# Reordering a few steps of a four-engine software pipeline: third tile's scale, two bias sums, third q's transpose, first z, and a score copy

## What is computed

```
# block 0: modulated linear, per-token attention among 16 heads of 32, modulated linear
kx = x @ (w * style * demod).T + b ; q = k = v = kx as (B, N, 16, 32)
A  = softmax(q @ k^T / sqrt(32))            # 16 x 16 for each token
x  = x + modulated_linear(A @ v)
# block 1: six normalised or shifted copies of x, one wide MLP, layer norm
h = ln(ln(x) * pw_g[id1] + pw_b[id1]) * cp_g[id2] + cp_b[id2] ; t, s = ln(x) * g[id] + b[id]
m, n, r = x + small MLPs of three conditioning vectors
x = x + ln(silu(concat(w0*h, w1*t, w2*m, w3*n, w4*r, w5*s) @ W1 + b1) @ W2 + b2) * g + be
```

## Time and profile before

| | |
|---|---|
| median of 3 runs | 898.75 us (898.54 to 901.41) |
| the profiled execution, its own time | 895.99 us |
| its span, first to last instruction | 894.2 us |
| TensorE busy | 849.9 us (95%) |
| VectorE busy | 699.7 us (78%) |
| GpSimd busy | 631.7 us (71%) |
| ScalarE busy | 482.4 us (54%) |
| mean granted TensorE clock | 0.984 of full speed |

### The profile page before, as it was taken

How to read it: one execution, slowest core, us unless ns; L and a number is a source line. 1 busy time by engine, 2 the same in 40 slices (tenths; PEclk the granted TensorE clock), 3 DMA queues, 4 the chain that set the end, 5 groups by cost and what they waited for, 6 DMA issues and landing times.

```text
span 894.2 us, 19747 instructions
## 1 busy us (share of the span) xinstructions
PE 849.9 (95%) x7456; PEld 770.7 (86%) x7474; DVE 699.7 (78%) x1099; ACT 482.4 (54%) x851; POOL 631.7 (71%) x766
## 2 busy tenths in 40 slices
PE   5996788999999999999999999999999999999987
PEld 5854777999899898999899898999899898999976
DVE  3687767779897878778897877789897877778642
ACT  3566446465555646465555646465555646464531
POOL 2458795868877776868878766868877776857661
PEclk9897999999999999999999999999999999999999
DMA  8961232434443341324444342434333342322110
GB/s 297 417 230 51 59 89 72 112 73 141 101 130 101 84 113 49 113 71 143 101 125 107 84 113 49 115 71 142 100 109 98 84 111 50 102 70 79 42 49 25
DMA packets 104367, 95.56 MB, mean 107 GB/s; under 512 B 72880, under 2 KB 78160, under 8 KB 102608
## 3 DMA queue, kind: packets, MB, share of 16 engines
q1 hardware_dynamic: 95056, 69.26, 26.8%
q0 software_dynamic: 4608, 16.78, 6.6%
q10 hardware_dynamic: 4608, 8.25, 2.7%
HBM read 69.60 MB, written 8.40 MB: 87 GB/s over the span
## 4 chain that ended last, share of the span: by engine, by line
PE 61%; DVE 16%; POOL 9%; issue 6%; ACT 4%; DMA 2%; ACTq 1%; SPq 0%; another core or an unknown queue 0%; DVEq 0%; POOLq 0%
PE acc L392 28%; PE tok L392 22%; PE att L392 5%; PE xp L545 4%; PE xp L392 2%; DVE Wkl L1151 2%; DVE SE L1288 1%; POOL op0l L1648 1%; DMA kb<-in_kb 1%; DVE op0l L1350 1%; DVE q L1251 1%; ACT L892 1%; DVE SE L1273 1%; DVE small L1284 1%; DVE xb L1312 1%
## 5 line engine op out<-in xcount | busy, mean ns | idle before, releaser
L1648 POOL TENSOR_TENSOR op1l<-ytmp,op1h 128x512 fp32r<-128x512 f32 x64 | 85.7, 1339 | 14.5 <-ACT op1h L880 13.9
L1594 POOL TENSOR_TENSOR xlo<-xraw,xhi 128x512 fp32r<-128x512 f32 x31 | 42.9, 1382 | 52.1 <-ACT xhi L775 52.1
L392 PE MATMUL acc<-op0h,W1xh 128*128 128x256 f32 x256 | 75.7, 296 | 3.8 <-DVE op0l L1330 3.4
L392 PE MATMUL acc<-op1h,W1th 128*128 128x256 f32 x256 | 75.6, 295 | 0.0
L880 ACT CAST op1h<-ytmp 128x512 fp32r<-128x512 f32 x64 | 39.7, 620 | 64.8 <-DVE ytmp L1344 64.8
L392 PE MATMUL acc<-op1h,W1hh 128*128 128x256 f32 x256 | 73.7, 288 | 0.0
L392 PE MATMUL acc<-op0h,W1sh 128*128 128x256 f32 x256 | 73.7, 288 | 0.0
L392 PE MATMUL acc<-op1l,W1th 128*128 128x256 f32 x256 | 73.1, 286 | 0.0
L392 PE MATMUL acc<-op1h,W1tl 128*128 128x256 f32 x256 | 73.1, 286 | 0.0
L392 PE MATMUL acc<-op1l,W1hh 128*128 128x256 f32 x256 | 72.4, 283 | 0.0
L392 PE MATMUL acc<-op0h,W1sl 128*128 128x256 f32 x256 | 72.4, 283 | 0.0
(11 more groups left out here) (262 smaller groups left out, 3177.5 us busy)
## 6 DMA issues: line engine op xcount, KB each, us to landing
xsq<-in_x SPq DMA_DIRECT2D x32, 256.0 KB, 3.1
xb<-in_x SPq DMA_DIRECT2D x32, 256.0 KB, 3.0
out<-xb SPq DMA_DIRECT2D x32, 256.0 KB, 2.1
BD<-q SPq DMA_DIRECT2D x124, 64.0 KB, 2.1
BD<-v SPq DMA_DIRECT2D x124, 64.0 KB
xraw<-in_xT SPq DMA_DIRECT2D x30, 256.0 KB, 2.9
ring<-in_k_wT ACTq DMA_DIRECT2D x6, 256.0 KB, 3.5
dmb<-dm_rows SPq DMA_DIRECT2D x6, 256.0 KB, 3.9
```

Of the source, the lines that this page charges most:

```text
L392: return e.matmul(o, a, b, start=start, stop=True, skip_group_check=True)
L1594: e.tensor_tensor(xlo[:, :, :], (xraw1 if g == 1 else xraw)[:, :, :], xhi[:, :, :].bitcast(F32), ALU.subtract).then_inc(s["xlo"], 1)
L1648: e.tensor_tensor(op[slot]["l"][:, :, half(g)], four(ytmp[YT[n, g][0]]), op[slot]["h"][:, :, half(g)].bitcast(F32), ALU.subtract).then_inc ...
```

## The change

Five edits, all of them of order; no instruction's work is changed, and one VectorE group is merged.

- ScalarE, start-up: `z_make(0)` stands ahead of `sum_part(1, "AV", "AVc")` and of the copy into `rv[0]`; before it stood behind both.
- VectorE, start-up: `q_T(2)` stands right behind `q_lo(2)`, ahead of `a_sum(1)`; one `x_weights(1, ..)` quarter that stood ahead of `a_sum(1)` now stands behind it.
- GpSimd, start-up: `true_scale(2)` stands ahead of the first three quarters of the W1 block h; before it stood behind them.
- GpSimd, step 1: `add_be(0)`, `add_be(1)` stand behind `root2(2)`; before they stood ahead of `true_scale(3)`.
- ScalarE, steps 1, 4, 8 and 12: `sum_part(b, "S", "Sc")` stands ahead of `z_make(a)` and `bias_2(pa)` (as it did in 3, 7, 11 and 15 already); and in step 1 `a_hi(2)` stands ahead of `prod_hi(0, "s")` and `u_make(1)`.

```diff
@@ scalar, start-up
+            z_make(0)
             sum_part(1, "AV", "AVc")
             e.wait_ge(s["Pm"], 15)
             e.copy(rv[0][:, :], mlp[:, :]).then_inc(s["Pc"], 1)
-            z_make(0)
@@ scalar, loop
-                if mod:
+                if mod or k == 1:
                     a_hi(a)
-                    if mod[1] == 1:
+                    if mod and mod[1] == 1:
                         mod_hi(*mod, (2, 3))
...
-                    if not mod:
+                    if not mod and k > 1:
                         a_hi(a)
...
-                    if mod and mod[1] == 0 or not more:
+                    if mod or not more or k == 1:
                         sum_part(b, "S", "Sc")
                         z_make(a)
                         bias_2(pa)
@@ vector, start-up
             q_lo(2)
-            x_weights(1, (1,))
+            q_T(2)
             a_sum(1)
-            q_T(2)
-            x_weights(1, (2,))
+            x_weights(1, (1, 2))
             a_lo(1)
@@ gpsimd, start-up
-            split_lo(W1["h", "l"], raw["h"], W1["h", "h"], None, range(3))
             true_scale(2)
+            split_lo(W1["h", "l"], raw["h"], W1["h", "h"], None, (0, 1, 2))
@@ gpsimd, loop
                 prod_lo(pb, "h")
-                if k == 1:
-                    add_be(0)
-                    add_be(1)
                 if front:
                     true_scale(b)
                     affine(a)
                     root2(a)
+                    if k == 1:
+                        add_be(0)
+                        add_be(1)
```

## The result

| | before | changed |
|---|---|---|
| median | 898.67 us (898.54 to 901.41, 4 runs) | 891.8 us (891.6 to 895.09, 4 runs) |
| ratio, 95% interval | | 0.9928, 0.9902 to 0.9954 |
| the profiled execution | 895.99 us, span 894.2 | 895.09 us, span 893.3 |

The changed kernel is 6.9 us faster (898.67 less 891.8; by the interval 4.1 to 8.8). The forecast was 893.6 us, 1.8 us above the measured median, and "faster by over 0.3%" had the largest chance.

What follows compares the result with a forecast made beforehand. TensorE was taken to be full after the start-up, leaving only waits in the start-up, step 1 and weight steps. Terms 1.5 + 2.3 + 1.3 = 5.1 us gave 893.6 us against the 898.75 median, range 890.3 to 897.8.

Steps and rivals of the forecast that it cites:

- Start-up, 1.5 us: Start-up to values of tile 2: 2.2 us lead from the earlier scale less 0.65 charged to GpSimd; bounds 0 and 3.5.
- about 1.6 us: Start-up: of 2.7 us less TensorE wait for q of tile 2, the part carried through VectorE to `less_max(2)`.
- `a_hi`: zero: Step 1: `a_hi` first removes a 0.95 us wait, but TensorE arrives earlier at the 1.60 us wait GpSimd sets; gain zero.
- Step 1, 2.3 us: Step 1: score copy first and bias sums later remove TensorE's whole 2.29 us wait for tile 3's softmax; bounds 1.1 and 2.3.
- at zero: Clock: the half-clock stretch near 139 us goes, one near 118 may come; netted to zero, 1.7 us each way.
- Weight steps, 1.3 us: Steps 4 and 12: score copy first removes the 0.69 and 0.65 us waits for `u_make`; step 8 gains nothing; bounds 0 and 1.5.
- the values of tile 3 before 136: Sign in step 1: values of tile 3, at 138.21 us before, come by 136, or the whole forecast falls.
- Values of tile 2 near 101.5: Sign in the start-up: TensorE's values of tile 2, at 103.28 us before, start near 101.5.
- Slower: Rival, start-up: the scale heads GpSimd's queue, waits for a late `less_max(2)` and delays work behind it; 3.9 us slower, 902.6; chance 0.06.
- Larger: Rival: L1288 gets in at the next boundary, `e_second` loses nothing, clock stays full at 138.7; 8.1 us, 890.7; chance 0.14.
- Smaller: Rival: VectorE's two-input instructions lose every boundary and the clock falls at 118 us; about 2.2 us, 896.5; chance 0.20.
- nothing: Rival: one engine's leads end at the next, GpSimd's total unchanged; only weight steps gain, 1.3 us, 897.4; chance 0.14.

Runs made afterwards that it cites:

- the repeat: The changed kernel, unaltered, timed again beside the kernel before: 894.81 us, ratio 0.995 (0.9927 to 0.9972), 4.5 us gained.
- added waits: Kernel before with one added wait holding GpSimd's second affine operation until VectorE's division is done in steps 4, 8 and 12: 897.27 us, 0.9979.

## Right and wrong, step by step

**The sum.** 1.5 + 2.3 + 1.3 = 5.1 us was forecast, 6.9 and 4.5 measured. By parts alone: scale with q and z 1.35 and nothing, step 1 3.6 (its interval is 2.1 to 5.1), weight steps 2.5 (1.35 to 3.7). The signs were right; by these intervals only the weight steps' term was short. That the sum came out is luck in part. By its terms the values of tile 3 should have come 3.8 us sooner, and they came 2.5 sooner from the anchor; what made up for it is the clock behind them and steps that the forecast held to be fixed, both below.

**Start-up, 1.5 us: reached at tile 2, hardly kept, and a step within it wrong.** The values of tile 2 came 1.62 us sooner from the anchor than in the trace of before, and 1.0 to 1.3 sooner than in the three others with its order. From the anchor to step 2 the first changed trace took 83.71 us and the repeat 82.62, but step 1's edits alone took 83.38, so at most 0.8 us of the lead was left there. The division got in at the next boundary, in 1.32 us, and `e_second` took 1.42, both as reckoned for the better case. What failed is "about 1.6 us" of VectorE brought forward by q's transpose. The scores did come about 2.5 us sooner against the anchor (6.04 us after it, 8.49 before), and the W1x split L1229 began 1.8 us sooner (17.91 against 19.69), but beside GpSimd's 5.46 us of W1s quarters it took 3.66 us where it had taken 2.50, and `less_max(2)` began at 94.39, 0.6 us sooner from the anchor. The lead was lost to the same blocking that the scale's edit was to avoid. The scale alone gave 1.19 of the 1.62. The charge of 0.65 us to GpSimd for two weight quarters side by side, 3.02 us for both (74.44), can't be told apart from that.

**The page's rule.** The Trainium skill (SBUF — State Buffer, "Who interferes with whom") says that the instruction issued first holds the shared ports for its whole length and the other blocks. Read as one instruction blocking one other once, it gave the start-up the lead of 3.3 us. The division (1.32) and `e_second` (1.42) agree; the 7.13, 3.72, 3.10 and 2.50 us rows don't, since each spans two to five GpSimd instructions, and the first of them had begun ahead of the five. The measurement decides: VectorE doesn't always get in when a GpSimd instruction ends and the next one follows. When it does and when it doesn't no run here settles.

**`a_hi`: zero, right,** and for the reason given: 0.95 became 0.50, and 1.60 became 2.67. The fear that went with it, that gathering two short waits brings a fall of the clock, isn't borne out: the fall is there without it too.

**Step 1, 2.3 us: right in kind, its size helped by the clock.** The values of tile 3 wait for nothing, and the scale came 3.3 us sooner. Step 1 shrank by 2.72 us alone, by 1.76 in the first trace of the whole and by 2.83 in its repeat. With step 1's edits alone the values of tile 3 come 66.75 us after the anchor, against 67.80 to 68.45 in the three traces with the old order (before, score copy, added waits): 1.1 to 1.7 us and not 2.3, since the wait at 118 had grown by 1.06 us. From there to step 2 it takes 16.63 us against 17.63 to 19.01, and in that stretch the three have a fall of the clock at 139 and this kernel has none. The forecast set a fall at 118 against the one at 139 "at zero". Both happened, and they weren't worth the same: the six kernels with the old order of step 1's bias sums have one at 137 to 146 and a step 1 of 62.5 to 63.9 us, those with the new order and W2 in its place have none there and 60.1 to 61.4, whether one or more falls lay ahead in it. A fall ahead of a wait may be partly absorbed by it; that is a reading, since order and fall changed together. With W2 moved there is a fall at 137 again and step 1 takes 58.9 to 60.3 us, so a fall there doesn't make a long step by itself. That the bias sums are a necessary part isn't borne out by the time of the whole: with them back, step 1 is 1.1 to 2.1 us longer and the tail 2.1 to 2.4 shorter.

**Weight steps, 1.3 us: mis-sized, 2.5 measured (1.35 to 3.7), and 1.8 by the traces.** "Step 8 gains nothing" was read from one execution in which step 8 happened to be short. Without the edit a step took 50.9 to 51.2 us in nine of twelve cases, and with it, in its own kernel and the changed one twice, 50.0 to 50.6; the means are 50.77 and 50.17, three times 0.6 us apart. The waits of 0.69 and 0.65 us are the part that TensorE shows. The step that failed is taking one execution's step for the usual one; three instances of it stood in the one trace, and they disagreed.

**The median and the trace.** Taking the gain from the median and not from the 895.99 us was right: the trace of before had step 8 short (0.8 us), no fall in the tail (2.3 us), and steps 2, 6 and 10 at 49.9, while in six traces with one part or none nine of these eighteen steps took 50.8.

**What the sum left out.** "In an ordinary step no reordering of another engine can gain anything" is a step of the prediction that failed: those steps have two lengths. In the seven traces of the changed kernel and of those with one piece taken back or W2 moved all twenty-one were short. An estimate from the means of the traces: 3.2 us up to step 2, 1.8 in the weight steps and 1.4 in steps 2, 6 and 10 (nine of eighteen, 0.93 us each, over six traces) make 6.4 us, between the two measurements of 6.9 and 4.5. Whether the changed order keeps these steps short or they came out so by chance was not tried.

**The marks set for it.** Met: the scores of tile 2, due at 75.6 and seen at 76.62, 0.82 of which the trace was late; `less_max(2)` at 0.69; the scale ahead of W1h, at 95.22 and later than said; no "DVE e" wait for tile 3; no wait in steps 4 and 12. Missed: "the values of tile 3 before 136", which came at 136.54, and by the forecast's own words it falls with that. The trace was 0.82 us late from the start, and from the anchor they moved from 68.45 to 65.96 us, 2.5 us, just enough for the mark; but the mark was looser than the sum, which had them at 134.4. "Values of tile 2 near 101.5" was missed by 1.0 us (102.48), mostly the late start.

**The rivals.** "Slower" had GpSimd blocked at the scale; it idled 1.50 us there, and 2.72 with the scale alone, of a slack of 3.9. "Larger" named what did occur at L1288, and its 8.1 us are nearer to the 6.9 than the forecast's 5.1, but farther from the repeat's 4.5; the two measurements don't tell the cases apart. "Smaller" (2.2 us) and "nothing" (1.3) are outside both intervals, 4.1 to 8.8 and 2.5 to 6.6 us.

## What to carry to other kernels

A VectorE instruction with two inputs in SBUF that meets a run of GpSimd instructions may wait for the whole run, so break up or move the run, and if need be make GpSimd wait. Before a term rests on one stage of one trace, look at the same stage's twins in that trace: if they disagree, price the average. Set marks relative to an event just ahead of the change, and expect that one fall of TensorE's clock can hide a saving of one or two us early on. A wait that is gone from a trace isn't a saving before the time of the row behind it has been compared too: the engine may only have come late.

## What the runs showed of the hardware

- Five GpSimd instructions in a row held one VectorE instruction of 0.75 us for 7.13 us; three held one of 0.69 us for 3.72. In the same kernels others got in after one, the division of tile 2 at 1.32 and 1.35 us.
- Adding three waits on GpSimd made a kernel faster, 0.9979 (0.9962 to 0.9996), and the one weight step of before in which a gather landed 0.46 us late was 0.8 us shorter than its twins.
- A fall of the clock, 4 us at 0.57, takes 1.7 us of TensorE's time (4.00 x 0.43); the longest here, 7.5 us at 0.54, takes 3.5. The same waits (0.7, 0.4 and 1.55 us in 6 us) were followed by one at 853 us in the changed kernel, and by none at the same place in the work in the trace of before. The Trainium skill (TensorE: Matmul & The Clock Gate, "What's actually happening") says that what the array did of late sets its clock, and the rows agree; they don't tell the two cases apart.
